# Full attention on one core: where the next unit's scores stand among the matmuls of the weighing of values

## The chip, the cores and the metric

One NeuronCore of a Trainium2 chip runs the whole program. The metric is the device time of that core in microseconds (us).

## The reference, cut to what matters

The model has two layers. Layer 0 is a time-mixing block followed by six layers of local attention with feed-forward. Layer 1 is full attention with a relative bias, followed by a mixture of eight experts. The change lies in the full attention of layer 1 alone:

```python
qkv = (x @ w_qkv.T).reshape(b, t, dh, 3, h).transpose(3, 0, 4, 1, 2)
q, k, v = qkv                      # b = 2, t = 1024, h = 16 heads, dh = 64
scores = einsum('bhid,bhjd->bhij', q, k) * scale + bias
attn = softmax(scores, axis=-1)
out = einsum('bhij,bhjd->bhid', attn, v)
out = out.transpose(0, 2, 1, 3).reshape(b, t, h * dh) @ w_out.T
```

## The kernel before, in words

The function `full_attention` works through 128 **units**. A unit is one pair of heads, one batch element and 128 queries against all 1024 keys: 8 pairs x 2 batch elements x 8 query blocks. Four units in a row make a **quad**. The values of a quad are weighed one quad later, in four steps s = 0 to 3, one step per unit.

Each engine runs its own loop over the iterations u (`STEPS`), and they meet through semaphores.

**TensorE** (loop at L1933). In iteration u, with s = u mod 4, it issues in this order:

- `scores(u + 1)` (L1859 to L1886): twelve matmuls of 64 rows x 512 columns at L1875, in two parts, into banks 0 to 3, and for the query blocks 6 and 7 some more for the bias (L1884). Banks 0 to 3 hold one unit's scores only, so part 0 waits until ScalarE has taken the exponents of unit u from banks 0 to 2 (semaphore `probs` at 3u + 2), and part 1 until it has done so with bank 3 (3u + 3).
- `wait_emptied(pe, u - 1)` (L1697): it waits until ScalarE has copied out what step u - 1 left in banks 4 to 7.
- at s = 0 two **jobs** (`job`, L1840: projections of the next half's queries, keys and values, L1851 and L1855).
- `weigh_v(q, s, 0)` and `weigh_v(q, s, 1)` (L1888): the two halves of the step's weighing, 64 small matmuls of 32 rows x 64 columns each at L1901, into banks 4 to 7.
- at s = 1 two output projections (`project_out`, L1925), at s = 2 and s = 3 two jobs, and at s = 2 also `spread_inverse` (L1916). At s = 1 and s = 2 the first of the two stands between the halves.

**ScalarE** (loop at L2040) in iteration u: `exponent(u + 1)` (one activation over 1024 columns at L2000 for the first head, two over 512 at L2006 for the second), then `wait_filled(act, u)`, then it copies out what step u left: the inverses (L2019) at s = 2, the two jobs (L1977 or L1981), the weighed values (L2024) at s = 3, the outputs (L2013) at s = 1. Then it rounds the jobs' results (L1990). So the copies that `wait_emptied(pe, u - 1)` waits for stand on ScalarE **behind** `exponent(u)`.

**VectorE** (loop at L2109): `maximum(u + 1)` (two reductions at L2078, after all twelve score matmuls of u + 1), then `turn(u)` (two transposes at L2088), and at s = 0 and 1 small work for the inverses.

**GpSimd** makes the low parts of queries and keys (L1788), divides (L1807) and adds to x (L1818). The **SP** queue loads weights and places the values (`place_v`, L1744). Neither is named by the change.

No planner is at work here: the order of each engine is written out by hand. The loop of TensorE around the change is:

```python
for u in STEPS:
    s, q = u % UPQ, weighed_at(u)        # q is None in the first quad
    fresh = s in (0, 3) or q is None
    if u + 1 < UNITS:
        scores(u + 1)
    wait_emptied(pe, u - 1)
    if s == 0:
        for j in jobs_at(u):
            job(j, fresh)
```

Jobs exist for u below 120; `scores(u + 1)` for u below 127.

Of the kernel before, what the change touches and what calls it, by code (L numbers as in the profile page):

```python
# [1599 lines left out]
def full_attention(nc, A, sb, sem, bank, ident, h_in, padded, x_chunk, mod):  # L1600
# [3 lines left out]
    UNITS = PAIRS * PER  # L1604
# [8 lines left out]
    with ExitStack() as ctx:  # L1613
# [46 lines left out]
        def lows_done(half, n):  # L1660

            return len(LOWS) * half + n
# [4 lines left out]
        def jobs_at(u):  # L1667
            q, s = u // UPQ, u % UPQ
            half = q // QPH + 1
            if s == 1 or half >= HALVES:  # L1670
                return []
            first = JPH * half + 6 * (q % QPH) + max(0, 2 * (s - 1))
            return [first, first + 1]

        def outs_at(u):
            q = u // UPQ - 2
            return [2 * q, 2 * q + 1] if u % UPQ == 1 and 0 <= q < QUADS else []

        def weighed_at(u):

            q = u // UPQ - 1
            return q if 0 <= q < QUADS else None
# [14 lines left out]
        def wait_emptied(eng, u):  # L1697

            if u < 0:
                wait_job_emptied(eng, JPH - 1)  # L1700
                return
            for j in jobs_at(u)[-1:]:
                wait_job_emptied(eng, j)
            for n in outs_at(u)[-1:]:
                eng.wait_ge(S.y, n + 1)
            q = weighed_at(u)
            if q is not None and u % UPQ == 2:
                eng.wait_ge(S.inv_out, q + 1)
            if q is not None and u % UPQ == 3:
                eng.wait_ge(S.att, q + 1)  # L1710
# [15 lines left out]
        with nc.Block(no_gpsimd_drain=True) as block:  # L1726
# [112 lines left out]
            def _(pe):  # L1839
                def job(j, start):  # L1840
                    half, i = j // JPH, j % JPH
                    kind, part = JOBS[i]
                    b = half % 2
                    if 4 <= j < JPH:
                        wait_job_emptied(pe, j - 4)
                    o = job_bank(j)
                    if i == 0:
                        pe.wait_ge(S.w_scaled, half // 2 + 1)
                    lo = PAD + part * JW
                    if kind < 2:  # L1850
                        mm = pe.matmul(o, w[:, half // 2 % 2, kind, :], h_in[:, b, lo:lo + JW], start=start, stop=True,  # L1851
                                       skip_group_check=True)
                    else:
                        for t in range(2):
                            mm = pe.matmul(o[:, t * P:(t + 1) * P], h_in[:, b, lo + t * P:lo + (t + 1) * P],  # L1855
                                           w[:, half // 2 % 2, 2, :], start=start, stop=True, skip_group_check=True)
                    mm.then_inc(S.proj, 1)

                def scores(u):  # L1859
                    half, qb = u // QB, u % QB  # L1860
                    b = half % 2
                    if qb == 0:
                        pe.wait_ge(S.low, lows_done(half, 5))
                    elif qb % 2 == 0:
                        pe.wait_ge(S.low, lows_done(half, 5 + qb // 2))
                    q = slice(qb * P, (qb + 1) * P)
                    for part in range(2):
                        near = qb >= 6 and part == 0
                        k = slice(part * CH, (part + 1) * CH)
                        if u >= 1:  # L1870
                            pe.wait_ge(S.probs, 3 * (u - 1) + 2 + part)
                        for n, (ql, kl) in enumerate(((qk_high, qk_high), (qk_high, qk_low), (qk_low, qk_high))):
                            for par in range(2):
                                f = slice(HD * par, HD * par + HD)
                                mm = pe.matmul(bank[:, 2 * par + part, :], ql[f, 0, b, q], kl[f, 1, b, k],  # L1875
                                               start=n == 0, stop=n == 2 and not near)
                        if near:
                            if qb == 6:
                                pe.wait_ge(S.rel_low, u // PER + 1)
                                pe.wait_ge(S.anti, 1)  # L1880
                            cols = slice(P, 2 * P) if qb == 6 else slice(0, 2 * P)
                            for n, r in enumerate((rel_high, rel_low)):
                                for par in range(2):
                                    mm = pe.matmul(bank[:, 2 * par, 0:P * (qb - 5)], anti[:, :], r[:, par, cols],  # L1884
                                                   start=False, stop=n == 1)
                    mm.then_inc(S.scores, 1)  # L1886

                def weigh_v(q, s, n):  # L1888

                    half = q // QPH  # L1890
                    lo, step = KB // UPQ * s, KB // UPQ // 2
                    if s == 0 and n == 0:
                        pe.wait_ge(S.turned, 2 * UPQ * (q + 1))
                        if q % QPH == 0:
                            pe.wait_ge(S.v, 256 * (half + 1))
                    for kb in range(lo + step * n, lo + step * (n + 1)):
                        for a in range(4):
                            rows = slice(32 * a, 32 * a + 32)
                            for par in range(2):
                                d = slice(HD * par, HD * par + HD)  # L1900
                                mm = pe.matmul(bank[d, 4 + a, 0:P].rearrange("p (u r) -> p u r", u=UPQ),  # L1901
                                               v[rows, half % 2, kb, d],
                                               prob_t[rows, q % 2, par, :, 32 * kb:32 * kb + 32],
                                               start=kb == 0, stop=kb == KB - 1, skip_group_check=True)
                    if n == 1:
                        mm.then_inc(S.av, 1)
# [13 lines left out]
                def project_out(n, start):  # L1920
                    q = n // 2
                    pe.wait_ge(S.att_t, q + 1)
                    if q % UPQ == 0:
                        pe.wait_ge(s_wo[q // UPQ % 2], 16 * (q // UPQ // 2 + 1))
                    pe.matmul(out_bank(n), w_out[:, q // UPQ % 2, :], att_t[:, q % 2, n % 2 * JW:n % 2 * JW + JW],  # L1925
                              start=start, stop=True, skip_group_check=True).then_inc(S.out, 1)
# [6 lines left out]
                for u in STEPS:  # L1933
                    s, q = u % UPQ, weighed_at(u)


                    fresh = s in (0, 3) or q is None
                    if u + 1 < UNITS:
                        scores(u + 1)
                    wait_emptied(pe, u - 1)  # L1940
                    if s == 0:
                        for j in jobs_at(u):
                            job(j, fresh)

                    outs, jobs = outs_at(u), jobs_at(u) if s >= 2 else []
                    if q is not None:
                        weigh_v(q, s, 0)
                        if s in (1, 2):
                            for n in outs[:1]:
                                project_out(n, fresh)  # L1950
                            for j in jobs[:1]:
                                job(j, fresh)
                            outs, jobs = outs[1:], jobs[1:]
                        weigh_v(q, s, 1)
                        if s == 2:
                            spread_inverse(q)
                    for n in outs:
                        project_out(n, fresh)
                    for j in jobs:
                        job(j, fresh)  # L1960
# [713 lines left out]
```

## Time and profile before

| | us |
|---|---|
| median of 3 runs | 2613.04 |
| lowest, highest | 2612.69, 2616.29 |
| the profiled execution's own time | 2625.65 |
| its span | 2623.9 |
| TensorE matmuls busy | 2453.0 (93%) |
| VectorE busy | 2159.1 (82%) |
| ScalarE busy | 2037.2 (78%) |
| GpSimd busy | 1518.5 (58%) |
| mean granted TensorE clock | 0.984 |

The span is the time from the first to the last instruction of the profiled execution; its own time is 1.75 us more. The full attention runs from about 1680 to 2414 us of the span. Matmuls overlap, so a row of TensorE that groups several gives the time from the start of the first to the end of the last, and from one row's start to the next row's start is what the group really takes. "Idle before" in square brackets is how long the engine stood still ahead of that row, and what ended it.

### The profile page before, as it was taken

Reading aid. Unit: us, or ns where it says so; the run is one execution under the profiler, and the core shown is the slowest. Engines: PE = TensorE matmul, PEld = TensorE weight load, DVE = VectorE, ACT = ScalarE, POOL = GpSimd, SP = SyncE. Lnnn points to the kernel's source line nnn. Section 1 sums busy time; section 2 is a strip of 40 time slices with the busy share of each in tenths; the row PEclk is TensorE's granted clock in tenths of the full one; section 3 lists DMA queues with packets and bytes.
Section 4 is the critical chain, followed back from the end, with each engine's and each line's share of the span. In section 5 each row is a group of like instructions: output and inputs, shape, how many; then the busy total and the mean of one; then the engine's idle time right before and its main releaser. Section 6 shows DMA issues by size and latency. Waiting matters only on the chain. (4 is left out here: it accounts for less than half of the span.)

```text
span 2623.9 us, 118567 instructions
## 1 busy us (share of the span) xinstructions
PE 2453.0 (93%) x52349; PEld 1966.4 (75%) x52349; DVE 2159.1 (82%) x2455; ACT 2037.2 (78%) x4077; POOL 1518.5 (58%) x1029
## 2 busy tenths in 40 slices
PE   6799999999999999999999999689999999997999
PEld 2488888888888888888888887467676776775787
DVE  5888888888888888888888887388888888885888
ACT  4688888889889888888888887566666666764676
POOL 3788887888788878888788785122222232322111
PEclk9899999999999999999999999899999999999999
DMA  3243433443334334333433333122222222221221
GB/s 96 56 94 92 106 77 92 92 106 83 93 93 113 80 89 102 96 83 93 97 94 79 85 85 71 36 54 52 60 61 58 50 61 60 57 53 34 82 73 41
DMA packets 275793, 202.01 MB, mean 77 GB/s; under 512 B 117568, under 2 KB 215880, under 8 KB 274248
## 3 DMA queue, kind: packets, MB, share of 16 engines
q1 hardware_dynamic: 275280, 194.42, 30.9%
q8 instruction: 414, 6.78, 1.1%
q14 instruction: 99, 0.81, 0.1%
HBM read 36.96 MB, written 1.11 MB: 15 GB/s over the span
## 5 line engine op out<-in xcount | busy, mean ns | idle before, releaser
L514 POOL TENSOR_TENSOR lt_t_sin<-lt_qk,lt_tab 128x512 f32<-128x512 f32 x384 | 682.8, 1799 | 243.9 <-DVE lt_qk L1296 241.8
L519 POOL TENSOR_TENSOR lt_qr<-lt_qr,lt_t_sin 128x1024 f32<-128x1024 f32 x192 | 457.8, 2385 | 28.2 <-POOL lt_t_sin L514 0.5
L2078 DVE TENSOR_REDUCE fa_neg_max<-bank 128x1 f32<-128x1024 f32 x256 | 301.6, 1220 | 94.7 <-PE bank L1875 93.3
L1901 PE MATMUL bank<-fa_prob_t,fa_v 32*64 32x128 f32 x16384 | 295.9, 277 | 18.9 <-issue 14.0
L2000 ACT ACTIVATE fa_prob<-bank,fa_neg_max 128x1024 f32<-128x1024 f32 x128 | 142.7, 1115 | 217.5 <-DVE fa_neg_max L2078 165.2
L1901 PEld LDWEIGHTS bank<-fa_prob_t,fa_v 32*64 32x64 f32 x16384 | 245.8, 131 | 81.3 <-issue 60.5
L2088 DVE STREAM_TRANSPOSE fa_prob_t<-fa_prob 128x1024 f32<-128x1024 f32 x256 | 302.1, 1219 | 0.0
L607 PE MATMUL bank<-lt_w_high,lt_x_high 128*128 128x512 f32 x576 | 262.8, 456 | 0.8 <-ACT lt_v_tok L1009 0.4
L1296 DVE TENSOR_TENSOR lt_qk<-lt_qk,lt_rn 128x2048 f32<-128x2048 f32 x96 | 236.3, 2461 | 5.9 <-ACT lt_rn L1003 2.2
L1289 DVE TENSOR_REDUCE lt_ssq<-lt_qr 128x32 f32<-128x2048 f32 x96 | 218.9, 2281 | 23.0 <-ACT lt_qr L985 23.0
L1303 DVE TENSOR_TENSOR lt_qr<-lt_qk,lt_tab 128x2048 f32<-128x2048 f32 x96 | 232.7, 2424 | 3.3
L977 ACT COPY lt_qk<-bank 128x512 f32<-128x512 f32 x384 | 220.4, 593 | 18.2 <-POOL lt_t_sin L514 2.8
L608 PE MATMUL bank<-lt_w_low,lt_x_high 128*128 128x512 f32 x576 | 228.4, 396 | 0.0
L609 PE MATMUL bank<-lt_w_high,lt_x_low 128*128 128x512 f32 x576 | 227.8, 396 | 0.0
L1316 DVE TENSOR_REDUCE lt_row_max<-bank 128x8 f32<-128x512 f32 x192 | 131.7, 686 | 113.4 <-PE bank L653 113.4
L624 PE MATMUL bank<-ident,lt_qr 128*128 128x128 f32 x1536 | 201.1, 274 | 14.7 <-POOL lt_qr L519 12.6
L985 ACT ACTIVATE lt_qr<-lt_qk 128x1024 f32<-128x1024 f32 x192 | 203.4, 1060 | 0.0
L624 PEld LDWEIGHTS bank<-ident,lt_qr 128*128 128x128 f32 x1536 | 177.5, 141 | 31.4 <-POOL lt_qr L519 15.7
L704 PEld LDWEIGHTS bank<-lt_prob_t,lt_w_o 128*128 128x128 f32 x1536 | 186.7, 192 | 8.1 <-issue 1.5
L704 PE MATMUL bank<-lt_prob_t,lt_w_o 128*128 128x128 f32 x1536 | 187.6, 275 | 1.0 <-ACT lt_prob_t L1035 0.8
L1807 POOL TENSOR_TENSOR fa_att_t<-fa_att,fa_inv_all 128x512 f32<-128x512 f32 x32 | 40.6, 1270 | 245.4 <-ACT fa_att L2024 245.4
L682 PEld LDWEIGHTS bank<-lt_v,lt_prob_t 64*32 64x32 f32 x12288 | 130.1, 105 | 66.7 <-issue 65.1
(260 smaller groups left out, 5912.5 us busy)
## 6 DMA issues: line engine op xcount, KB each, us to landing
lt_v<-lt_v_tok SPq DMA_DIRECT2D x576, 128.0 KB
fa_v<-fa_v_tok SPq DMA_DIRECT2D x256, 128.0 KB, 2.7
lt_v<-lt_v_tok SPq DMA_DIRECT2D x192, 64.0 KB
lt_k_t<-lt_k_t SPq DMA_DIRECT2D x84, 128.0 KB, 2.7
lt_v<-lt_v SPq DMA_DIRECT2D x168, 64.0 KB, 2.1
lt_w_raw<-in_lt_wqkv_dram SPq DMA_DIRECT2D x36, 256.0 KB
ex_cw_all<-cw_kept SPq DMA_DIRECT2D x8, 1024.0 KB, 4.5
lt_x_s<-h_in SPq DMA_DIRECT2D x96, 64.0 KB, 2.7
```

Of the source, the lines that this page charges most:

```text
L514: pool.tensor_tensor(dst[:, :, i, :], src[:, :, 1 - i, :], tab[:, g // 2 % 2, 1, at:at + 32].unsqueeze(1).to_broadcast([P, HEADS, 32]), AL ...
L519: pool.tensor_tensor(qr[:, g % 2, half], qr[:, g % 2, half], t_sin[:, :], ALU.add).then_inc(S.rotated, 1)
L607: pe.matmul(o, xh, w_high[:, k % WS, :], start=True, stop=False)
L608: pe.matmul(o, xh, w_low[:, k % WS, :], start=False, stop=False)
L609: return pe.matmul(o, xl, w_high[:, k % WS, :], start=False, stop=True)
L624: mm = pe.transpose(bank[:, turn_bank("turn", g, j), n * P:(n + 1) * P], qr[:, g % 2, (4 * j + n) * P:(4 * j + n + 1) * P], ident[:, :])
L704: mm = pe.matmul(o, w_o[:, layer % 2, hp, :], att_t[:, g % 2, hp, :], start=hp == 0, stop=hp == PAIRS - 1)
L1296: dve.tensor_tensor(heads, heads, r.unsqueeze(2).to_broadcast([P, 2 * HEADS, HD]), ALU.mult)\
L1303: dve.tensor_tensor(qr[:, g % 2, :].rearrange("p (a h d) -> p a h d", a=2, h=HEADS), qk[:, g % 2, :].rearrange("p (a h d) -> p a h d", a=2 ...
L1901: mm = pe.matmul(bank[d, 4 + a, 0:P].rearrange("p (u r) -> p u r", u=UPQ), v[rows, half % 2, kb, d], prob_t[rows, q % 2, par, :, 32 * kb:3 ...
L2078: dve.tensor_reduce(neg_max[:, u % 2, par:par + 1], bank[:, 2 * par:2 * par + 2, :].rearrange("p a n -> p (a n)"), AX.X, ALU.max, negate=T ...
L2088: dve.transpose(prob_t[:, q % 2, par, u % UPQ, :], prob[:, u % 2, par, :]).then_inc(S.turned, 1)
```

## The change

On TensorE, in iterations with s = 0 or s = 3 in which values are weighed, `scores(u + 1)` no longer stands at the head of the iteration, but between the two halves of the weighing. At s = 1 and s = 2, and in the first quad, it stays at the head. No instruction is added or taken away, and the other engines' orders are the same.

```diff
                     fresh = s in (0, 3) or q is None
-                    if u + 1 < UNITS:
+                    between = s in (0, 3) and q is not None
+                    if u + 1 < UNITS and not between:
                         scores(u + 1)
                     wait_emptied(pe, u - 1)
                     if s == 0:
...
                     if q is not None:
                         weigh_v(q, s, 0)
+                        if u + 1 < UNITS and between:
+                            scores(u + 1)
                         if s in (1, 2):
```

## Rows read from the trace of the kernel before

**Rows 1.** Stretch: us, then busy PE, PEld, DVE, ACT, POOL, clock, DMA share, GB/s
```profile
2000.00:2100.00 100.00, 96.36 (x2739) 70.77 (x2740) 88.29 (x93) 70.23 (x181) 27.90 (x37) 1.00 0.27 61
```

**Rows 2.** Waits within 1720 to 2385 us: who waited for whom, total, times, longest
```profile
PEld bank L1875 <- ACT fa_prob L2006: 25.1, 51, 1.5
...
PE bank L1901 <- issue: 13.5, 16, 1.5
...
PE bank L1875 <- ACT fa_prob L2006: 11.6, 32, 1.3
```

**Rows 3.** Timeline, steps s = 0 and 1: start, us, engine, line, [idle before]
```profile
2049.75 0.50 PE L1875 MATMUL bank<-fa_qk_high 64*128 64x512 f32 x2 [0.19 <-ACT fa_prob L2006]
...
2050.26 0.65 ACT L1977 COPY fa_raw<-bank 128x256 f32<-128x256 f32 x2
...
2050.78 0.62 ACT L2024 COPY fa_att<-bank 128x512 f32<-128x512 f32 x1
...
2051.45 2.36 DVE L2078 TENSOR_REDUCE fa_neg_max<-bank 128x1 f32<-128x1024 f32 x2 [0.30 <-PE bank L1875]
...
2051.49 1.10 PE L1851 MATMUL bank<-h_in,fa_w 128*128 128x256 f32 x4
...
2052.53 2.09 PE L1901 MATMUL bank<-fa_prob_t,fa_v 32*64 32x128 f32 x128
...
2054.52 0.68 ACT L2006 ACTIVATE fa_prob<-bank,fa_neg_max 128x512 f32<-128x512 f32 x1
...
2054.77 0.49 PE L1875 MATMUL bank<-fa_qk_high 64*128 64x512 f32 x2
...
2055.19 0.64 ACT L1977 COPY fa_raw<-bank 128x256 f32<-128x256 f32 x2
```

**Rows 4.** Timeline, steps s = 2 and 3, up to the next s = 0
```profile
2059.86 0.50 PE L1875 MATMUL bank<-fa_qk_high 64*128 64x512 f32 x2
...
2061.45 1.21 PE L1901 MATMUL bank<-fa_prob_t,fa_v 32*64 32x128 f32 x64
...
2064.57 0.70 PE L1851 MATMUL bank<-h_in,fa_w 128*128 128x256 f32 x2
...
2065.20 0.50 PE L1875 MATMUL bank<-fa_qk_high 64*128 64x512 f32 x2
...
2065.31 0.59 ACT L2019 COPY fa_inv_all<-bank 128x512 f32<-128x512 f32 x1
...
2065.79 0.65 ACT L1977 COPY fa_raw<-bank 128x256 f32<-128x256 f32 x2
...
2066.79 2.10 PE L1901 MATMUL bank<-fa_prob_t,fa_v 32*64 32x128 f32 x128
...
2070.14 0.49 PE L1875 MATMUL bank<-fa_qk_high 64*128 64x512 f32 x2 [0.19 <-ACT fa_prob L2006]
```

**Rows 5.** Timeline, the last unit (no scores left to compute)
```profile
2392.20 0.58 ACT L2019 COPY fa_inv_all<-bank 128x512 f32<-128x512 f32 x1
...
2392.83 3.54 PE L1901 MATMUL bank<-fa_prob_t,fa_v 32*64 32x128 f32 x128 [2.16 <-ACT fa_inv_all L2019]
```

**Rows 6.** Timeline, first units of the stage, after idle time on TensorE
```profile
1694.24 1.13 PE L1851 MATMUL bank<-h_in,fa_w 128*128 128x256 f32 x4 [2.21 <-ACT fa_v_tok L1981]
...
1700.33 0.79 PE L1875 MATMUL bank<-fa_qk_high 64*128 64x512 f32 x2 [2.29 <-ACT fa_prob L2006]
...
1703.30 2.36 DVE L2078 TENSOR_REDUCE fa_neg_max<-bank 128x1 f32<-128x1024 f32 x2 [1.64 <-PE bank L1875]
...
1717.48 0.80 PE L1875 MATMUL bank<-fa_qk_high 64*128 64x512 f32 x2 [2.19 <-ACT fa_prob L2006]
```

**Rows 7.** Stretches of half a us: us, PE busy, granted clock, DMA share, GB/s
```profile
1700.50:1701.00 0.50, 0.50 (x4) 0.50 0.80 170
...
1717.50:1718.00 0.50, 0.50 (x2) 0.50 0.00 0
...
2393.50:2394.00 0.50, 0.50 (x36) 0.50 0.00 0
```

## The prediction

> **What bounds the kernel now.** I read the table of stretches first, then the waits of the full attention, then its timeline unit by unit. In the steady part of the stage TensorE is busy 96% of the time at the full clock (1.00, which is the 2.4 GHz level), VectorE 88%, ScalarE 70% [rows 1]. So matmuls fill the stage, and the reader should see how little is idle: of some 665 us, the first matmul or weight load of the scores waits 11.6 and 25.1 us for ScalarE's exponents, and the weighing stands still 13.5 us for nothing that the trace names [rows 2].
>
> The timeline shows why this works. Scores of one unit start at 2049.75, of the next at 2054.77 [rows 3]: 5.02 us. Between them TensorE issues the scores (1.74 to the jobs, 1.59 where the weighing follows at once, 2059.86 to 2061.45 [rows 4]), two jobs (1.04) and two halves of weighing (2.24, so 1.12 each) [rows 3]. In the same 5 us another chain runs round: VectorE's reductions start 1.70 after the scores start (2051.45), then come the exponents, whose third activation starts at 2054.52; the next scores may start when the second is done, some 4.95 after the last start (the interval in which they are seen to wait for it is 2065.20 to 2070.14, 4.94 [rows 4]). Both loops are as good as equal. That chain leaves TensorE about 3.3 us per unit, and today every unit brings between 3.3 and 3.7 us of other work to fill it.
>
> ScalarE copies banks 4 to 7 out behind the exponents: the copies start at 2055.19, 5.44 after the scores of that unit started, and take 1.14 at s = 3 (2050.26 to 50.78 + 0.62) [rows 3] and 1.13 at s = 2 (2065.31 to 65.79 + 0.65) [rows 4]. Today this wait stands behind the scores: they hold TensorE until 2051.49 and 2066.79, when the copies have ended at 2051.40 and 2066.44. **The scores are the cover of that wait.** Where they are not there, it shows: with the last unit the copy ends at 2392.78, and the weighing starts at 2392.83, after 2.16 us of idleness [rows 5].
>
> **The change, part by part.** No instruction is added. The move is made past `wait_emptied`, the jobs of s = 0, and one half of weighing. TensorE issues no DMA in this part, so no transfer moves with it; SP's placing of values and GpSimd's low parts hang on exponents and copies that only come later.
>
> *s = 3.* Count from the start of the scores of s = 2. They, one half, a job, the other half, the inverses and a job are done at 5.34 (2059.86 to 2065.20 [rows 4]). The copies of s = 2 end at 5.44 + 1.13 = 6.57; the half starts 0.05 later, 6.62; the scores behind it start at 7.74. Before it was 5.34: **+2.40**. For query block 7 both become longer by the same bias matmuls.
>
> *s = 0.* Count from the start of the scores of s = 3. Now a half (1.12) and two jobs (1.04) stand behind them, so TensorE is through at 3.75. The copies of s = 3 end at 5.44 + 1.14 = 6.58, plus 0.05; then two jobs (1.04) and a half (1.12): the next scores start at 8.79. Before 4.94: **+3.85**. VectorE's transposes of the unit before, for which this half also waits, start behind the reductions (1.70 + 2.36) and take about as long, 6.42: the copies come later and decide.
>
> *s = 1.* Only a half of weighing is left ahead of these scores; they wait for the exponents and start after 4.95 to 5.02, as before: 0. TensorE stands idle some 2.1 us (1.59 + 1.2 to 4.95). *s = 2.* Unchanged, 5.09 (2054.77 to 2059.86): 0. The moved scores cost nothing in themselves: scores to weighing is 1.59 where scores to jobs was 1.74, and I book no gain for it because those steps are bound by the wait.
>
> *Count.* s = 0 with weighing and scores: u = 4 to 124, 31 times; s = 3: u = 7 to 123, 30 times. Where no jobs are left, from u = 120 on, less is waited for: at 120 the jobs of s = 0 fall away (2.8), at 123 and 124 the copy is 0.58 [rows 5] alone, 5.44 + 0.58 + 0.05 + 1.12 = 7.19 against 4.94 (2.25 each). So 29 x 3.85 + 2.8 + 2.25 + 29 x 2.40 + 2.25 = 188.6 us.
>
> *Given back.* The unnamed stalls in the weighing, 13.5 us [rows 2], fall on any half. Four of the eight halves of a quad will have idle time behind them (the second of s = 0 and s = 3, both of s = 2), so half of it is hidden: -6.7. Bounds 0 and -13.5.
>
> *The clock.* The stage's new idle gaps are about 2.1 us ahead of the scores at s = 1 and 2.9 us (3.75 to 6.63) ahead of the jobs at s = 0; the one at s = 3 is 1.3 us. After gaps of 2.29 and 2.19 us the matmuls ran at the lower level [rows 6], granted clock 0.50, which is 1.2 GHz [rows 7]; the 2.16 us of the last unit were followed by it too, and 128 weighing matmuls took 3.54 us where 2.09 is usual [rows 5, 3]; after 2.21 us two pairs of jobs kept their 1.1 us [rows 6]. So three of four gaps of this size brought it. A slow spell costs what scores show: VectorE starts 2.97 after them (1700.33 to 1703.30) [rows 6] against 1.70, so 1.27. No row has this rhythm of gaps. Bounds: never, 0; after both long gaps of every quad and also slowing the rest of the step, 1.45 each (3.54 - 2.09), 62 x 1.45 = +90. I take half of the 2.1 us gaps, as they are a little shorter than those three, and seven tenths of the 2.9 us ones: 31 x 1.2 x 1.27 = **+47**. The Trainium skill, in "TensorE: Matmul & The Clock Gate", section "Why this matters for your kernels", asks only that idle gaps between bursts stay below a length that both of these stay below; by it the clock would hold and the sum be without this term, about 2795. The trace does not agree: [rows 5 to 7] show the fall after shorter gaps.
>
> *Sum.* 188.6 - 6.7 + 47 = +229. The durations are from the profiled execution (own time 2625.65, span 2623.9), which lies 12.6 us above the median of 2613.04; I add to the median: **2842 us**, 8.8% slower.
>
> **The rivals.**
> (a) *The clock holds* and only the late copies count: +182, 2795 us. For it: the gap of 2.21 us without a fall, and that TensorE, with about 20.4 us of work (5.02 + 5.09 + 5.34 + 4.94) in a quad of 26.6, would still be busy three quarters of the time. Against it: three of four gaps. Chance 0.27.
> (b) *The copies cost nothing, only uneven filling does.* If the halves started without waiting for step u - 1, s = 1 would still have 1.59 + 1.12 of work for a loop of 4.95, and 2.2 us of TensorE's full time would be lost per quad: 31 x 2.2 = 68, 2681 us. For it: today the wait never shows ahead of these steps. Against it: the code puts the copies behind `exponent(u)`, and [rows 5] show the wait bare. Chance 0.05.
> (c) *Not slower.* The half of weighing fills the time in which the scores now wait for exponents, and the copies are there in time. Its place is `wait_emptied` at s = 0 and s = 3; its price the waits of scores in [rows 2], at most 11.6 + 25.1, of which about half fall at these steps: -18, 2595 us. It decides only if the copies end before 4.95 after the scores' start; they end at 6.57 and 6.58. Chance 0.02.
> (d) *The clock falls after nearly every long gap*, and slows jobs and halves too: +182 + 90 = 2885 us. Chance 0.16.
> (e) *No change*, as the steps are bound elsewhere: it would need the exponents, not TensorE's order, to set the pace everywhere. Chance 0.01.
> My forecast, 2842 us with the clock falling after part of the gaps, has 0.49.
>
> **How the numbers follow.** The range reaches from case (a) with all stalls hidden and shorter waits than I read, 2785, to case (d), 2885. Below it lie (b), (c), (e) and a part of (a); above it a part of (d). About 0.2% (5 us) is what a measurement of this kernel can tell from no change. Faster: (c), 0.02; the same: (e), 0.01; slower: the others, 0.97.
>
> **What would show it.** In the profile after, the first exponents (L2000) of a quad's four units start 5.0, 5.1, 7.7 and 8.8 us apart instead of 5.0, 5.1, 5.3 and 4.9. TensorE's idle time ahead of the first half at s = 3 and of the jobs at s = 0 is ended by ScalarE's copies (L1977, L1981, L2024), 30 x 1.3 + 31 x 2.9, about 129 us; ahead of the scores at s = 1 by the exponents (L2006), 65 us. VectorE's wait for the scores grows by about 230 us, as its own work stays the same. TensorE's busy share in the stage falls from 96% to about 75%, and its clock to between 0.85 and 1. The forecast is wrong if `wait_emptied` ends nothing at s = 0 and 3 (then b or c), and its last term if the stage's clock stays at 1.00 (a).

## The result and the profile after

The change makes the kernel **11.4% slower**: 2922.61 us (median of 4 runs, 2902.22 to 2928.05) against 2614.66 us before (4 runs, 2612.69 to 2626.99); ratio 1.1144, 95% interval 1.1098 to 1.1191. Run once more in another sitting it took 2932.71 us against 2625.72 (1.1188, 1.1141 to 1.1235). The forecast was 2842 us, with a range up to 2885: the sign was right, the size too small by some 80 us. The profiled execution took 2902.22 us, so its rows show the least of the loss.

The page of the changed kernel, first the busy times, then the granted clock in 40 slices, then two of the costliest groups (busy, mean ns of one, idle before and what ended it):

```profile
PE 2577.3 (89%) x52349; PEld 2052.4 (71%) x52349; DVE 2156.6 (74%) x2455; ACT 2035.0 (70%) x4077; POOL 1518.7 (52%) x1029
...
PEclk9899999999999999999999889988888888988899
...
L2081 DVE TENSOR_REDUCE fa_neg_max<-bank 128x1 f32<-128x1024 f32 x256 | 301.6, 1220 | 381.6 <-PE bank L1875 381.3
...
L1901 PE MATMUL bank<-fa_prob_t,fa_v 32*64 32x128 f32 x16384 | 342.5, 302 | 51.0 <-ACT fa_v_tok L1984 18.4
```

The counts of instructions are those of before. VectorE and ScalarE work as long as before and wait longer: the reductions (L2078 before, L2081 now) wait 381.6 us for scores. TensorE's matmuls, though the same ones, are busy 124 us longer, and the clock is lower from where the full attention begins (1680 us lies in slice 24). Outside this stage the kernel is not slower: the stage's first exponent starts at 1680.1 us (1691.4 before), and from its last one to the end it is 235.1 us (234.2).

The steady stretch that answers to [rows 1], with the same columns:

```profile
2000.00:2100.00 100.00, 80.54 (x1848) 59.13 (x1853) 58.26 (x62) 46.07 (x119) 18.78 (x25) 0.81 0.13 30
```

The waits between 1720 and 2670 us (who waited for whom: total, times, longest), against [rows 2]:

```profile
DVE fa_neg_max L2081 <- PE bank L1875: 359.8, 119, 7.0
...
PE bank L1875 <- ACT fa_prob L2009: 67.1, 31, 2.2
...
PE bank L1851 <- ACT fa_raw L1980: 39.4, 14, 2.8
PE bank L1855 <- ACT fa_att L2027: 38.0, 14, 2.9
...
PE bank L1901 <- ACT fa_v_tok L1984: 18.4, 15, 1.2
PE bank L1901 <- ACT fa_raw L1980: 17.2, 14, 1.2
...
PE bank L1901 <- issue: 1.2, 2, 0.8
```

Here are the waits that the forecast named. Ahead of the jobs at s = 0 (L1851, L1855) TensorE now waits for ScalarE's copies, 28 times, 2.7 to 2.8 us each; ahead of the first half at s = 3 (L1901) 29 times, 1.2 us; ahead of the scores at s = 1 for the exponents, 31 times, 2.2 us. Before, the matmuls showed neither of the first two. The last line is what is left of the unnamed stalls of the weighing, 13.5 us before.

The timeline of one quad, in the columns of [rows 3]. First the wait at s = 3, which answers to the last rows of [rows 4]:

```profile
2194.03 0.58 ACT L2022 COPY fa_inv_all<-bank 128x512 f32<-128x512 f32 x1
...
2194.51 0.66 ACT L1980 COPY fa_raw<-bank 128x256 f32<-128x256 f32 x2
...
2195.22 1.21 PE L1901 MATMUL bank<-fa_prob_t,fa_v 32*64 32x128 f32 x64 [1.23 <-ACT fa_raw L1980]
...
2196.36 0.50 PE L1875 MATMUL bank<-fa_qk_high 64*128 64x512 f32 x2
```

Copies, 0.05 us, half (1.14), scores: as worked out. Then s = 0 and s = 1, one quad later:

```profile
2236.21 0.62 ACT L2027 COPY fa_att<-bank 128x512 f32<-128x512 f32 x1
...
2236.93 2.04 PE L1851 MATMUL bank<-h_in,fa_w 128*128 128x256 f32 x4 [2.81 <-ACT fa_raw L1980]
...
2238.91 2.01 PE L1901 MATMUL bank<-fa_prob_t,fa_v 32*64 32x128 f32 x64
...
2240.85 0.79 PE L1875 MATMUL bank<-fa_qk_high 64*128 64x512 f32 x2
...
2243.63 2.36 DVE L2081 TENSOR_REDUCE fa_neg_max<-bank 128x1 f32<-128x1024 f32 x2 [7.03 <-PE bank L1875]
...
2246.94 0.79 PE L1875 MATMUL bank<-fa_qk_high 64*128 64x512 f32 x2 [2.22 <-ACT fa_prob L2009]
...
2249.91 2.36 DVE L2081 TENSOR_REDUCE fa_neg_max<-bank 128x1 f32<-128x1024 f32 x2 [1.36 <-PE bank L1875]
```

The order is the foreseen one and the wait ends where it should, but what follows it is slow: two jobs take 1.98 us instead of 1.04, the half 1.94 instead of 1.12, and from the scores to VectorE's start it is 2.78 instead of 1.70. Together 2.84 us more in one step. The scores of s = 1 are slow as well, 2.97. The granted clock says why (the figures are: length of the stretch in us, TensorE's busy time and its count, clock, DMA share, GB/s):

```profile
2233.50:2234.00 0.50, 0.50 (x3) 1.00 0.00 0
2236.00:2236.50 0.50, 0.00 (x0) 0.89 0.65 179
2237.00:2237.50 0.50, 0.50 (x2) 0.50 0.82 176
2242.50:2243.00 0.50, 0.50 (x4) 0.50 0.00 0
2243.50:2244.00 0.50, 0.50 (x34) 1.00 0.00 0
```

It fell to the 1.2 GHz level while TensorE still stood idle ahead of the jobs, and came back only when the scores were nearly done. In quads of the query blocks 4 to 7, where the scores of s = 1 carry bias matmuls, the half behind them is slow as well (1.93 us from 2217.16 to 2219.09, instead of 1.14), and the scores of s = 2 start late.

### The profile page after: what moved, and what is told of

It is laid out like the page before. It is cut to its first block and busy times, and to the rows that moved or that the text cites. A ratio compares the mean times of both kernels' runs of the same rounds, so it can differ in the third digit from the quotient of the medians.

```text
span 2900.4 us, 118567 instructions
## 1 busy us (share of the span) xinstructions
PE 2577.3 (89%) x52349; PEld 2052.4 (71%) x52349; DVE 2156.6 (74%) x2455; ACT 2035.0 (70%) x4077; POOL 1518.7 (52%) x1029
## 5 line engine op out<-in xcount | busy, mean ns | idle before, releaser
L2081 DVE TENSOR_REDUCE fa_neg_max<-bank 128x1 f32<-128x1024 f32 x256 | 301.6, 1220 | 381.6 <-PE bank L1875 381.3
L1901 PE MATMUL bank<-fa_prob_t,fa_v 32*64 32x128 f32 x16384 | 342.5, 302 | 51.0 <-ACT fa_v_tok L1984 18.4
L1901 PEld LDWEIGHTS bank<-fa_prob_t,fa_v 32*64 32x64 f32 x16384 | 275.1, 144 | 142.7 <-issue 81.6
L1875 PE MATMUL bank<-fa_qk_high 64*128 64x512 f32 x512 | 144.6, 557 | 77.7 <-ACT fa_prob L2009 76.8
L1788 POOL TENSOR_TENSOR fa_qk_low<-fa_raw,fa_qk_high 128x256 fp32r<-128x256 f32 x128 | 90.5, 727 | 212.2 <-ACT fa_qk_high L1993 211.4
```

Source lines behind the costliest of these rows:

```text
L2081: dve.tensor_reduce(neg_max[:, u % 2, par:par + 1], bank[:, 2 * par:2 * par + 2, :].rearrange("p a n -> p (a n)"), AX.X, ALU.max, negate=T ...
```

## The experiments

Each time is a median of 4 runs. A "step" below is the time from one unit's first exponent to the next unit's, named by the s of the iteration that computes the next unit's scores. The first four were run together, with 2624.67 us for the kernel before (7 runs, 2612.12 to 2631.01), the last three together, with 2625.72 (7 runs, 2614.9 to 2631.99). "Loss" is against the kernel before of the same sitting.

| kernel | us | loss | ratio to before (95%) | mean clock |
|---|---|---|---|---|
| s3_only | 2686.67 | 62.0 | 1.0247 (1.0211 to 1.0283) | 0.982 |
| s0_only | 2780.70 | 156.0 | 1.0601 (1.0556 to 1.0647) | 0.964 |
| wait_first | 2722.31 | 97.6 | 1.0373 (1.0334 to 1.0413) | 0.973 |
| fill_ab | 2797.53 | 172.9 | 1.0671 (1.0633 to 1.0708) | 0.986 |
| fill_b | 2847.44 | 221.7 | 1.0858 (1.0817 to 1.0899) | 0.963 |
| fill_a | 2846.74 | 221.0 | 1.0845 (1.0803 to 1.0887) | 0.967 |
| after_again (the change) | 2932.71 | 307.0 | 1.1188 (1.1141 to 1.1235) | 0.933 |

The clock is that of the profiled execution over its whole span; before it was 0.984.

### s3_only: between the halves at s = 3 alone

```diff
-                    between = s in (0, 3) and q is not None
+                    between = s == 3 and q is not None
```

> The scores stand between the halves at s = 3 only; at s = 0 they are at the head again. Theory (the copies decide): the step from the scores of s = 2 to those of s = 3 takes 7.74 us instead of 5.34, the other three as before, so 30 x 2.40 = 72 us more than before, 2687 us. Only one idle gap of TensorE per quad, 1.3 us, so the clock stays at 1.00. Rival (uneven filling alone): 5.34 + 1.12 = 6.46, the step after it 4.95, so 30 x 1.12 = 34 us more, 2648 us.

Measured: 2686.67 us. The first exponents of s3_only around one quad (start in us, then its length):

```profile
2258.48 1.11 ACT L2003 ACTIVATE fa_prob<-bank,fa_neg_max 128x1024 f32<-128x1024 f32 x1 [2.68 <-DVE fa_neg_max L2081]
...
2266.32 1.12 ACT L2003 ACTIVATE fa_prob<-bank,fa_neg_max 128x1024 f32<-128x1024 f32 x1 [4.20 <-issue]
...
2271.22 1.11 ACT L2003 ACTIVATE fa_prob<-bank,fa_neg_max 128x1024 f32<-128x1024 f32 x1 [0.71 <-DVE fa_neg_max L2081]
...
2276.23 1.12 ACT L2003 ACTIVATE fa_prob<-bank,fa_neg_max 128x1024 f32<-128x1024 f32 x1 [1.29 <-DVE fa_neg_max L2081]
...
2281.34 1.11 ACT L2003 ACTIVATE fa_prob<-bank,fa_neg_max 128x1024 f32<-128x1024 f32 x1 [1.81 <-DVE fa_neg_max L2081]
```

The step of s = 3 is 7.84 us (the working gave 7.74, uneven filling alone 6.46), the other three 4.90, 5.01 and 5.11 as before. The copies decide. The loss of 62 us is 10 less than 30 x 2.40, and the trace shows where: in sum the steps of s = 3 are 75 us longer than before, but those of s = 0 and s = 1 are 7.5 and 3.5 us shorter, because irregular long steps are gone (TensorE's unnamed stalls in the weighing fell from 13.5 to 4.2 us). The clock is 1.00 in two of three stretches of 100 us and 0.98 in the third (1800 to 1900, 2000 to 2100, 2200 to 2300 us): one spell at the lower level, which began 0.8 us after a gap of only 1.23 us.

### s0_only: between the halves at s = 0 alone

```diff
-                    between = s in (0, 3) and q is not None
+                    between = s == 0 and q is not None
```

> The scores stand between the halves at s = 0 only. Theory (the copies decide): from the scores of s = 3 to those of s = 0 8.79 us instead of 4.94, the others as before, so 29 x 3.85 + 5 = 117 us more, 2732 us with the clock at 1.00. TensorE now stands idle 1.8 us ahead of the jobs at s = 0 (4.87 to 6.63) and 2.1 us ahead of the scores at s = 1; if these gaps, too, bring the clock down, up to 31 x (1.3 to 2.8) more, 2770 to 2820 us. Rival (uneven filling alone): 4.87 + 1.04 + 1.12 = 7.03 instead of 4.94, 2679 us.

Measured: 2780.70 us, so 156 us of loss where the copies at full clock account for 117. A quad's step of s = 0, then that of s = 1, where the clock held:

```profile
2283.06 1.11 ACT L2003 ACTIVATE fa_prob<-bank,fa_neg_max 128x1024 f32<-128x1024 f32 x1 [1.55 <-issue]
...
2291.84 1.11 ACT L2003 ACTIVATE fa_prob<-bank,fa_neg_max 128x1024 f32<-128x1024 f32 x1 [4.60 <-DVE fa_neg_max L2081]
...
2296.85 1.11 ACT L2003 ACTIVATE fa_prob<-bank,fa_neg_max 128x1024 f32<-128x1024 f32 x1 [1.29 <-DVE fa_neg_max L2081]
```

The step of s = 0 is 8.78 us, the worked-out 8.79. Two of these steps took 3.5 us and more above that, seven 0.9 to 1.5. The other 39 us go with spells of the lower clock: 25 begin between 1720 and 2500 us, 16 of them behind the idle gap of 2.2 us ahead of the scores at s = 1, 10 of these when TensorE had been back at work for over a us. Uneven filling (2679) is out.

### wait_first: only the wait is moved

```diff
                     if u + 1 < UNITS and not between:
                         scores(u + 1)
                     wait_emptied(pe, u - 1)
+                    if u + 1 < UNITS and between:
+                        scores(u + 1)
...
                         weigh_v(q, s, 0)
-                        if u + 1 < UNITS and between:
-                            scores(u + 1)
```

> At s = 0 and s = 3 the scores stand behind the wait for the copies, but ahead of the jobs and of both halves: the wait alone is moved. Theory: the scores start when the copies end, 6.62 us after the ones before at s = 3 (5.34 before) and 6.63 at s = 0 (4.94 before), so 30 x 1.28 + 31 x 1.69 = 91 us more than before, 2706 us; idle gaps 1.3 and 1.8 us, clock near 1.00. The rest of the loss of the change at full clock, 188 - 91 = 97 us, is then the half (and the jobs) ahead of the scores. Rival (the copies cost nothing): no change, 2615 us.

Measured: 2722.31 us, 97.6 us of loss for 91 worked out. The steps of s = 3 and s = 0 in one quad:

```profile
2142.99 1.11 ACT L2003 ACTIVATE fa_prob<-bank,fa_neg_max 128x1024 f32<-128x1024 f32 x1 [2.69 <-DVE fa_neg_max L2081]
...
2149.69 1.11 ACT L2003 ACTIVATE fa_prob<-bank,fa_neg_max 128x1024 f32<-128x1024 f32 x1 [2.85 <-issue]
...
2156.29 1.11 ACT L2003 ACTIVATE fa_prob<-bank,fa_neg_max 128x1024 f32<-128x1024 f32 x1 [2.42 <-DVE fa_neg_max L2081]
```

They are 6.7 and, where the clock held, 6.6 us. 16 spells of low clock, all short, lie in the loss as well; the steps of s = 1 alone are 9.3 us longer in sum than in fill_ab below. At full clock the wait by itself adds 1.3 us at s = 3 and 1.7 us at s = 0 (5.4 and 4.9 before), about half of what the change adds there (7.8 and 8.8 in fill_ab below); what is put between the wait and the scores adds the rest.

### fill_ab: matmuls of zeros in both long gaps

The added matmuls multiply a block of zeros, 7 at the end of s = 0 and 9 at its head; they add nothing to any result, and the rest of the computation is whole. The lines that make the zeros and wait for them are left out here:

```diff
+                def fill(n, o, start):
+                    for _ in range(n):
+                        pe.matmul(o, idle_w[:, :], ident[:, :], start=start, stop=True, skip_group_check=True)
...
+                    if s == 0 and between and u + 1 < UNITS:
+                        pe.wait_ge(S.probs, 3 * u + 1)
+                        fill(9, bank[:, 0, 0:P], True)
                     wait_emptied(pe, u - 1)
...
                     for j in jobs:
                         job(j, fresh)
+                    if s == 0 and q is not None and u + 1 < UNITS:
+                        fill(7, bank[:, 6, P:2 * P], False)
```

> The change, with matmuls of a block of zeros put into both long idle gaps of TensorE: 7 at the end of s = 0 (ahead of the scores of s = 1), 9 at the head of s = 0 (ahead of the wait for the copies); their results are not used. Some 0.26 us each, so 1.8 and 2.4 us of gaps of 2.1 and 2.9. Theory (the clock falls in these gaps, and that is what the forecast priced too low): the granted clock of the stage returns to 1.00, the quad to 8.79 + 5.0 + 5.1 + 7.83, the time to 2790 to 2805 us, over 110 us faster than the change, though more is computed. Rival (something else stretches the matmuls of s = 0 and s = 1, or zeros do not count as work for the clock): no gain or slower, 2915 us or more.

Measured: 2797.53 us. **With more work for TensorE the kernel is 125 us faster than the change** (2922.61, another sitting; 135 against its repetition). The stretches that answer to [rows 1] in fill_ab:

```profile
1800.00:1900.00 100.00, 92.77 (x2354) 70.46 (x2338) 71.40 (x76) 54.66 (x140) 23.20 (x32) 1.00 0.19 41
2000.00:2100.00 100.00, 92.09 (x2332) 69.60 (x2336) 68.87 (x74) 52.98 (x136) 22.03 (x30) 0.98 0.23 50
```

The added matmuls stand where the gaps were, with 0.41 us of idle time left ahead of the first group (a row of 18 is 9 matmuls, as each leaves two records):

```profile
2240.89 2.27 PE L1932 MATMUL bank<-ident,fa_idle_w 128*128 128x128 f32 x18 [0.41 <-ACT fa_prob L2015]
...
2248.19 1.83 PE L1932 MATMUL bank<-ident,fa_idle_w 128*128 128x128 f32 x14
```

The clock is back at 1.00 (one spell is left between 1720 and 2500 us). First exponents of fill_ab around one quad, and then the changed kernel's around a quad with the same query blocks:

```profile
2239.63 1.11 ACT L2015 ACTIVATE fa_prob<-bank,fa_neg_max 128x1024 f32<-128x1024 f32 x1 [4.20 <-issue]
...
2248.42 1.11 ACT L2015 ACTIVATE fa_prob<-bank,fa_neg_max 128x1024 f32<-128x1024 f32 x1 [4.62 <-DVE fa_neg_max L2093]
...
2253.43 1.11 ACT L2015 ACTIVATE fa_prob<-bank,fa_neg_max 128x1024 f32<-128x1024 f32 x1 [1.28 <-DVE fa_neg_max L2093]
...
2258.55 1.11 ACT L2015 ACTIVATE fa_prob<-bank,fa_neg_max 128x1024 f32<-128x1024 f32 x1 [1.81 <-DVE fa_neg_max L2093]
...
2266.38 1.11 ACT L2015 ACTIVATE fa_prob<-bank,fa_neg_max 128x1024 f32<-128x1024 f32 x1 [3.60 <-issue]
```

```profile
2233.27 1.11 ACT L2003 ACTIVATE fa_prob<-bank,fa_neg_max 128x1024 f32<-128x1024 f32 x1 [3.99 <-issue]
...
2244.89 1.11 ACT L2003 ACTIVATE fa_prob<-bank,fa_neg_max 128x1024 f32<-128x1024 f32 x1 [7.45 <-DVE fa_neg_max L2081]
...
2251.17 1.11 ACT L2003 ACTIVATE fa_prob<-bank,fa_neg_max 128x1024 f32<-128x1024 f32 x1 [2.56 <-DVE fa_neg_max L2081]
...
2256.39 1.11 ACT L2003 ACTIVATE fa_prob<-bank,fa_neg_max 128x1024 f32<-128x1024 f32 x1 [1.92 <-DVE fa_neg_max L2081]
...
2264.22 1.11 ACT L2003 ACTIVATE fa_prob<-bank,fa_neg_max 128x1024 f32<-128x1024 f32 x1 [3.60 <-issue]
```

Filled, the steps of s = 0 to 3 are 8.79, 5.01, 5.12 and 7.83 us; the prediction had 8.8, 5.0, 5.1 and 7.7. Unfilled they are 11.62, 6.28, 5.22 and 7.83. Nearly the whole difference lies in the first two (in the quads of the query blocks 4 to 7 the third is 0.9 us longer too, 6.89), and it goes with the clock.

### fill_b and fill_a: one gap filled

fill_b keeps only the 9 matmuls at the head of s = 0, fill_a only the 7 at its end; the rest of the edit is as above.

> The change, with the 9 matmuls of zeros at the head of s = 0 alone (ahead of the wait for the copies). Theory: the spell at half clock that stretched jobs, half and scores of s = 0 (11.6 instead of 8.8 us) is gone in nearly all of 31 quads, which is 2.8 us each where it came; the one ahead of the scores of s = 1 can stay, 1.3 us a quad. So 2800 to 2845 us. Rival (any long gap costs alike, both the same): about the middle between the change and both filled, 2860 us.

> The change, with the 7 matmuls of zeros at the end of s = 0 alone (ahead of the scores of s = 1). Theory: the gap of 2.9 us ahead of the jobs of s = 0 still brings the clock down in most quads, and costs 2.8 us there: 2797 + 25 x 2.8 = 2867 us, up to 2885. Rival (both gaps cost alike): 2860 us or less; if the two spells only come together, near 2800.

> The change itself once more, beside the two runs with one filled gap each. Theory: 2900 to 2930 us, with the long steps of 11.5 us behind the wait for the copies wherever the clock fell ahead of the jobs of s = 0, and 8.8 us where it did not.

Measured: 2847.44 and 2846.74 us, and 2932.71 for the change beside them. All three expectations were missed: fill_b lies 2 us above its range, fill_a 20 us below its figure, the change 3 us above its range. With one gap open it costs 50 us, whichever it is, against 135 us for both together (2932.71 - 2797.53). "Both cost alike" had given 2860: right that they are alike, 13 us too high. The steps show two different reasons for the same sum. A long step of s = 0 in fill_a:

```profile
2304.40 1.11 ACT L2012 ACTIVATE fa_prob<-bank,fa_neg_max 128x1024 f32<-128x1024 f32 x1 [3.58 <-issue]
...
2316.06 1.11 ACT L2012 ACTIVATE fa_prob<-bank,fa_neg_max 128x1024 f32<-128x1024 f32 x1 [6.96 <-DVE fa_neg_max L2090]
```

A long step of s = 1 in fill_b:

```profile
2069.76 1.11 ACT L2013 ACTIVATE fa_prob<-bank,fa_neg_max 128x1024 f32<-128x1024 f32 x1 [4.17 <-DVE fa_neg_max L2091]
...
2077.39 1.11 ACT L2013 ACTIVATE fa_prob<-bank,fa_neg_max 128x1024 f32<-128x1024 f32 x1 [4.51 <-DVE fa_neg_max L2091]
```

In fill_a a spell touched the step of s = 0 in 19 of 30 quads. 9 of these steps were 2.7 to 2.8 us longer than in fill_ab (11.6 instead of 8.8), and there the clock fell while TensorE stood idle ahead of the jobs; of the other 10, most some 1.5 us longer, 6 had the fall up to 1 us after the jobs had begun. In fill_b the spells touched 15 quads, nearly all with the query blocks 4 to 7, where the scores of s = 1 and s = 2 carry the bias matmuls and the spell stretches the first and delays the second (7.62 and 7.0 instead of 5.81 and 6.00).

Not tried: the change with the wait behind the first half. That half writes the banks which ScalarE is then still copying, at s = 0 the very columns, so there the wait can only be moved together with what follows it. At s = 3 they are other columns of the same banks; whether the kernel could do without the wait there is open.

## Why the prediction was wrong, point by point

**What bounds the stage, and that the scores cover the wait:** right. wait_first moves nothing but that cover and loses 97.6 us.

**s = 3, +2.40, and s = 0, +3.85:** right to 0.1 us each (s3_only: 7.84; fill_ab: 8.79). **s = 1 and s = 2 unchanged:** right at full clock (5.01 and 5.12). **The moved scores cost nothing in themselves:** right by the same figures.

**The count, 188.6, less 6.7 for hidden stalls:** 182 against 172.9 of loss in fill_ab. The copies' term was right, the one for stalls too small. Before, the 13.5 us of unnamed stalls lay within single steps of s = 0 (8.5 us in eight steps of 5.6 to 6.3 us instead of 4.9), s = 1 and s = 2; in fill_ab 1.6 us of them are left, in the change 1.2. So some 12 us were hidden, not half, and 188.6 - 12 = 177 lies near the 175 us by which the steps of fill_ab are longer than those before.

**The clock, +47: the step that failed.** In the prediction's words, "a slow spell costs what scores show: ... so 1.27", and "I take half of the 2.1 us gaps ... and seven tenths of the 2.9 us ones". In the profiled execution of the change the steps of 30 quads are 105 us longer than the same steps of fill_ab in sum, 61 at s = 0, 30 at s = 1 and 14 at s = 2 (the whole executions differ by 2902.22 - 2796.14 = 106); by medians it is 125 to 135. Taking a step as touched where it is 0.9 us or more longer than in fill_ab, s = 0 was touched in 25 of 30 quads and s = 1 in 19. So 44 steps were touched where 31 x 1.2 = 37 falls were assumed, and the clock's own record has 46 spells between 1720 and 2600 us: the count was a little low. The price was the error: 105 / 44 = 2.4 us instead of 1.27. I had priced the scores alone, but behind the 2.9 us gap everything on the path up to VectorE's start is slow: jobs +0.94, half +0.82, scores +1.08, 2.84 us in one go. Behind the 2.2 us gap the scores alone cost the 1.27 where there are no bias matmuls (6.28 instead of 5.01), but 1.8 us with them (7.62 instead of 5.81), and 0.9 more at s = 2. My upper bound of 1.45 per spell was not one, for it also took a single group of matmuls, and so case (d), which took both gaps every time, still came out at 2885.

**The rivals.** (a), clock holds, 2795 us: that is the time of fill_ab, 2797.5, where the clock is made to hold; the change itself does not do so. The rule of the Trainium skill ("TensorE: Matmul & The Clock Gate", section "Why this matters for your kernels"), weighed there, speaks for a held clock. These traces do not agree: gaps of 2.2 us, 2244.72 to 2246.94 among them, ended at the lower level. (b), uneven filling alone: out by s3_only and s0_only. (c), faster: out, as the copies end 6.6 us after the scores' start in the change too. (d) was nearest, with too low a price for too many falls.

**What would show it:** the waits by name came as listed: 28 x 2.8 and 29 x 1.2 us for copies, 31 x 2.2 for exponents. VectorE's wait grew by 381.6 - 94.7 (its page of before) = 287 us instead of 230, by the clock term. TensorE's busy share in the steady stretch fell to 81% and not to 75, as its matmuls took longer. The stage's clock was 0.81 to 0.93 in stretches of 100 us and 0.85 over 1720 to 2670 us, where 0.85 to 1 was forecast.

## What to carry to other kernels

An instruction that stands ahead of a wait may be the wait's cover: before moving it behind, look up when the waited-for work ends and count from there, not from the engine's own load. Where a change opens idle gaps like these (2.2 and 2.8 us) on TensorE inside a loop, price the lower clock over everything on the path behind the gap, not over one operation, and look how often the loop's rhythm brings the gap back. If such a gap can't be closed, idle matmuls in it can be worth their place: here they gave back 125 us of 308, and the order before is still 173 us better.

## What was not expected of the hardware

**Long and short spells.** Read in quarters of a us, the 46 spells at the lower level in the change's stage (1720 to 2600 us) lasted either 3.25 to 3.5 us (18) or 6.75 to 7.0 us (28), and none in between. All the long ones began while TensorE still stood idle, 0.44 to 0.88 us before its work came back (for instance 2202.25 to 2209.00, with work back at 2203.07). Of the short ones none began earlier than 0.40 us before it, and several when work was already back (for instance 1748.25 to 1751.75). In the stage of s0_only two long ones and in that of fill_b three began after the work had come back, so this describes the change and is no rule.

**A loop that locks in.** From about 1940 to 2390 us the quads of the change repeat to 0.1 us (11.62, 6.28, 5.22, 7.83, then 11.54, 7.63, 6.89, 7.84), with the clock falling in every one of the long gaps; earlier and later some of these gaps bring no fall. Two gaps per quad cost 135 us by medians, each alone 50. By the steps of the profiled executions it is 105 us (116 in after_again) against 38 (fill_a) and 42 (fill_b). So the two together cost more than the sum of each alone. Why is not settled.
